# Counting gathered rows by half supersteps in the second edge loop of a two-layer graph network

## The chip, the cores and the metric

The kernel runs on one core of a Trainium2 chip. The metric is the time of one execution on the device in microseconds (us), lower is better. PE is the matrix engine (PEld its weight loads), DVE the vector engine, ACT the scalar engine, POOL the GpSimd engine, which here issues the indirect DMAs, and SP the engine that issues plain DMAs.

## What is computed

200,000 edges, sorted by destination, run between 12,500 nodes of 64 features. Cut to what matters, the reference is:

```
# layer 0
msg = relu(concat([x[dst], x[src], edge_attr, u[0]]) @ W1 + b1)
agg = segment_sum(msg, dst)
x   = layernorm(x + relu(concat([x, agg, u[0]]) @ W2 + b2))
# layer 1, 8 kinds of edges
Z   = einsum('ni,rio->nro', x, fc_weight)
e   = relu(sum(concat([Z[src, etype], Z[dst, etype]]) * attn_weight[etype]))
ex  = exp(e - segment_max(e, dst)[dst])
h   = segment_sum(ex / segment_sum(ex, dst)[dst] * Z[src, etype], dst)
x   = layernorm(x + h)
```

## The kernel before

**Tiles, slots, supersteps.** The edges are cut into NT = 1563 tiles of P = 128. The nodes are cut into NB = 98 blocks of 128. A tile whose edges end in more than one block is worked on once for each block; each such pair of a tile and a block is a slot. O = 8 slots are a superstep, and each loop runs over SO = 208 of them. The destinations that the reference draws make 1658 slots; the last six are filled up with the last tile. So the tile in the last slot of a superstep moves on by 8 from one superstep to the next, less one for every block that ends in between: counted from the drawn destinations it is tile 1510, 1517, 1525, 1532, 1539, 1546, 1553, 1560 and 1562 for supersteps 199 to 207.

**The two loops.** `phase_layer0` is the first loop, `phase_layer1` the second; `phase_mid` between them makes the tables of the second, and `phase_out` writes the result. In both, POOL runs `gathers`: for each tile in order one indirect DMA fetches the 128 source rows (table `Btab` or `Ztab`) into a ring of RING = 184 tiles, 23 supersteps' worth. POOL waits for the consumers only where a place of the ring is used again: for `used` and `summed`, which are PE's and DVE's progress some ten supersteps back.

**The count of landed rows.** In `gathers`, tiles are counted by eights (tiles 8g to 8g+7 are group g). Each gather adds 16 to one of four semaphores `s_g`, by its group. After the issue of the fourth tile of group g+1, `counted(g)` waits until all of group g has landed and adds 1 to the semaphore `landed`:

```
if s and j == min(3, NT - s * O - 1):
    counted(s - 1)
```

**Who waits for it.** A table `xrow` has four words for each superstep; word 0 is the group of the last slot's tile, plus 1. In the first loop DVE waits for it in `filled`. In the second PE waits for it in `scores(s)`, behind the first of 16 small matmuls into p_e:

```
if j == 0:
    e.wait_ge(S["landed"], e.snap(xreg, min_val=1, max_val=TO))
```

PE's order in one pass s of the second loop is `turned(s-1)` (p_x, from ACT's ohe), `scores(s+1)` (p_e), half of `summed(s-3)` (p_s from ohx), `spread(s-1)` (p_s from m), the other half of `summed(s-3)`. DVE does `scores`, `onehots(s+2)`, `maxima(s-1)`, `sums(s-4)`, `shifted(s-2)`. The tables `brow`, `wrow`, `xrow` are made once at the head of the first loop: DVE computes rows of `rowsf`, PE transposes them, DVE casts them to whole numbers.

Of the kernel before, what the change touches and what calls it, by code (L numbers as in the profile page):

```python
# [5 lines left out]
F32 = mybir.dt.float32  # L6
BF16 = mybir.dt.bfloat16
I32 = mybir.dt.int32
ALU = mybir.AluOpType
# [4 lines left out]
P = 128  # L14
# [7 lines left out]
NT = -(-E // P)  # L22
O = 8
TO = -(-NT // O)
# [4 lines left out]
SC = NS // P  # L29
# [46 lines left out]
CHUNKS = [(q, q + QC) for q in range(0, NQ, QC)]  # L76
# [356 lines left out]


ECHO = 8


def echoes(e, ping, echo, first):
# [4 lines left out]
            e.sem_inc(echo, 1)  # L443


def gathers(e, A, ring, table, idx, s_g, landed, used, summed, ping=None, echo=None, first=NT, free={}):

    tiles = lambda s: min(NT - s * O, O)


    def counted(s):
        e.wait_ge(s_g[s % len(s_g)], 16 * sum(tiles(i) for i in range(s % len(s_g), s + 1, len(s_g))))
        e.sem_inc(landed, 1)  # L453

    for t in range(NT):
        s, j = divmod(t, O)
        if s in free and j == 0:
            e.wait_ge(*free[s])
        if s >= RT and j == 0:
            e.wait_ge(used, s - RT + BEHIND + 1)  # L460

        if s >= RT and j in (2, 4, 6):
            e.wait_ge(summed, O * (s - RT + BEHIND - 1) + j)
        if j % 4 == 1 and t > first:
            e.wait_ge(echo, ECHO * ((t - first) // 4 + 1))
        e.indirect_dma_start(out=ring[:, place(t), :], out_offset=None, in_=table[:, :],  # L466
                             in_offset=bass.IndirectOffsetOnAxis(ap=idx[:, t:t + 1], axis=0)).then_inc(s_g[s % len(s_g)], 16)
        if j % 4 == 0 and t >= first:
            e.sem_inc(ping, 1)
        if s and j == min(3, NT - s * O - 1):  # L470
            counted(s - 1)
    counted(TO - 1)


def rows_loaded(e, A, drow, s_dr, made, g):
# [8 lines left out]
def phase_layer0(nc, A):  # L484

    QE, QO = 2, 3
    EARLY = 10 * O
    H = O // 2
    with ExitStack() as ctx:
# [3 lines left out]
        ring = sb("ring0", [P, RING, D], F32)  # L493
# [12 lines left out]
        xTA = ring[:, XT0:RING, :].rearrange("p (q h) d -> p q (h d)", h=2)  # L506

        rA = OH[:, :, :, :].rearrange("p a j k -> p (a j k)")[:, 0:2 * QC * 2 * D].rearrange("p (a q h d) -> p a q h d", a=2, q=QC, h=2)
        rowsf = sb("rows_f", [P, 6, SC], F32)

        rowi = msg[0:SC, :, :, :].rearrange("p a j d -> p (a j d)")[:, 0:3 * P + PER * WX].bitcast(I32)
        rowx = rowi[:, 3 * P:3 * P + PER * WX].rearrange("p (s w) -> p s w", w=WX)
# [16 lines left out]
        pre, tot = pM[:, 3, 256:256 + SC], pM[:, 3, 288:288 + SC]  # L529
        tab = pM[:, 3, P:P + 4 * SC].rearrange("p (m v) -> p m v", v=4)  # L530
        pR = pM[0:SC, 0, :].rearrange("p (r k) -> p r k", r=4)
        pR2 = pM[0:SC, 1, 0:2 * P].rearrange("p (r k) -> p r k", r=2)
        pL = [pM[:, 1 + i, :].bitcast(BF16).rearrange("p (m k) -> p m k", k=P) for i in range(2)]
        pY = lambda g: pM[:, 3 if g % 2 == 0 else 0, :].rearrange("p (m k) -> p m k", k=P)
        A3v = A.A3[:, 0:NB, :].rearrange("p (q h) c -> p q h c", h=2)
# [32 lines left out]

        @block.gpsimd
        def _(e):  # L570
            gathers(e, A, ring, A.Btab, idx, s_g, S["landed"], S["full"], S["acc"], S["ping"], S["echo"], EARLY, {XT0 // O: (T["a"], len(CHUNKS))})

        @block.scalar
        def _(e):
# [82 lines left out]
        def _(e):  # L657
# [49 lines left out]
            for r in range(4):  # L707
                e.transpose(pR[:, r, :], rowsf[:, r, :], A.ident[:, :])
            e.wait_ge(T["dh"], 8)
            for r in range(2):  # L710
                last = e.transpose(pR2[:, r, :], rowsf[:, 4 + r, :], A.ident[:, :])
            last.then_inc(T["rowt"], 1)
            multiplied(2)
# [44 lines left out]
        def _(e):  # L758
            breg = [e.alloc_register(f"l0vb{j}") for j in range(O)]
            treg = [e.alloc_register(f"l0vt{j}") for j in range(O)]  # L760
            xreg = [e.alloc_register(f"l0vx{j}") for j in range(WX)]
            done = Chain(e, T["dve"])
            c13 = lambda v: v.unsqueeze(2)

# [44 lines left out]
            done(e.tensor_scalar(out=rowsf[:, 5, :], in0=rowsf[:, 1, :], scalar1=float(O), scalar2=float(O), op0=ALU.is_ge, op1=ALU.mult))  # L809
            done(e.tensor_tensor(out=rowsf[:, 4, :], in0=rowsf[:, 5, :], in1=rowsf[:, 1, :], op=ALU.subtract))  # L810
            done(e.tensor_tensor(out=rowsf[:, 4, :], in0=rowsf[:, 4, :], in1=rowsf[:, 2, :], op=ALU.add))
            done(e.tensor_scalar(out=rowsf[:, 0, :], in0=tab[:, :, 1], scalar1=A.kcol[:, 0:1], scalar2=float(NB), op0=ALU.add, op1=ALU.min))
            done(e.tensor_scalar(out=nb128[:, :], in0=rowsf[:, 0, :], scalar1=-float(P), scalar2=None, op0=ALU.mult))
            e.sem_inc(T["rows"], 1)
# [8 lines left out]
            e.tensor_copy(rowx[:, :, 0:1], by(pR[:, 3, :])[:, :, O - 1:O])  # L823
            e.tensor_copy(rowx[:, :, 1:2], by(pR2[:, 0, :])[:, :, O - 1:O])
            e.tensor_copy(rowx[:, :, 2:3], by(pR2[:, 1, :])[:, :, O - 1:O])
            e.memset(rowx[:, :, 3:4], 0).then_inc(T["rowi"], 1)
            remainder(0)
            remainder(1)
            e.wait_ge(A.s_typ, 32)
# [38 lines left out]
                e.tensor_tensor(out=acc, in0=acc, in1=pS[s % 2][:, j:j + 1, :], op=ALU.add).then_inc(S["acc"], 1)  # L868

            def filled(s):  # L870
                e.wait_ge(S["landed"], e.snap(xreg[0], min_val=1, max_val=TO))
                if s:
                    e.wait_ge(S["pre"], s)
                of, to = e.snap(xreg[1], min_val=0, max_val=RING - O), e.snap(xreg[2], min_val=0, max_val=O)
                e.tensor_tensor(out=full[:, bass.ds(to, O), :], in0=owns, in1=ring[:, bass.ds(of, O), :], op=ALU.add).then_inc(S["full"], 1)  # L875
# [11 lines left out]
            for s in range(SO + 2):  # L887
                if s + 1 < SO:
                    onehots(s + 1)
                if s < SO:  # L890
                    if s:
                        e.wait_ge(S["msg"], s)
                    for h in range(2):
                        e.wait_ge(S[f"m{h}"], s + 1)
                        e.tensor_reduce(out=pT[:, h * H:(h + 1) * H, :], in_=half(h), axis=AXX, op=ALU.add).then_inc(T["dve"], 1)  # L895
                if s >= 2:
                    e.reg_load(breg, A.brow[0:1, (s - 2) * O:(s - 1) * O])
                if s < SO:
                    e.reg_load(xreg, xrow[0:1, s, :])
                    e.reg_load(treg, wrow[0:1, s, :])  # L900
                    filled(s)
                    take(e, T["dve"], 2)
                for j in range(O):
                    if s >= 2:
                        summed(s - 2, j)
                    if s < SO:
                        added(s, j)
# [341 lines left out]
def phase_layer1(nc, A):  # L1249

    QO, QT, QV = 7, 5, 4
    with ExitStack() as ctx:
# [42 lines left out]

        @block.gpsimd
        def _(e):
            gathers(e, A, ring, A.Ztab, idx, s_g, S["landed"], S["s"], S["acc"])

        @block.scalar  # L1300
        def _(e):
# [22 lines left out]
        @block.tensor  # L1324
        def _(e):
            breg = [e.alloc_register(f"l1pb{j}") for j in range(O)]
            treg = [e.alloc_register(f"l1pt{j}") for j in range(O)]
            ureg = [e.alloc_register(f"l1pu{j}") for j in range(O)]
            xreg = e.alloc_register("l1px")

            def scores(s):
                e.reg_load(breg, A.brow[0:1, s * O:(s + 1) * O])
                e.reg_load(treg, trow[0:1, s, :])
                e.reg_load(xreg, xrow[0:1, s, 0:1])
                e.wait_ge(S["oht"], s + 1)
                if s:
                    e.wait_ge(S["ev"], s)
                for j in range(O):
                    b = e.snap(breg[j], min_val=0, max_val=NB)
                    e.matmul(pE[:, j, :], OHT[:, s % QT, j, :], A.S23[:, bass.ds(b, 1), :], start=True, stop=False)  # L1340
                    if j == 0:
                        e.wait_ge(S["landed"], e.snap(xreg, min_val=1, max_val=TO))
                    t = e.snap(treg[j], min_val=0, max_val=RING - 1)
                    part = ring_s[:, bass.ds(t, 1), 2 * D + 2:2 * D + 5].rearrange("p a i -> p (a i)")
                    last = e.matmul(pE[:, j, :], A.ident_h[:, :], part.unsqueeze(2).to_broadcast([P, 3, R]), start=False, stop=True)  # L1345
                last.then_inc(S["e"], 1)

            def turned(s):
                e.wait_ge(S["ohe"], s + 1)
                for j in range(O):  # L1350
                    last = e.transpose(pX[:, j, :], OHe[:, s % 2, j, :], A.ident[:, :])  # L1351
                last.then_inc(S["x"], 1)

            def spread(s):
                e.wait_ge(S["m3"], s + 1)
                for j in range(O):
                    last = e.matmul(pB[s % 2][:, j, :], OHT[:, s % QT, j, :], m3[:, s % 2, j, :], start=True, stop=True)
                last.then_inc(S["b"], 1)

            def summed(s, h):  # L1360
                if h == 0:
                    e.reg_load(ureg, trow[0:1, s, :])
                    e.wait_ge(S["ohx"], s + 1)
                for j in range(4 * h, 4 * h + 4):
                    t = e.snap(ureg[j], min_val=0, max_val=RING - 1)
                    last = e.matmul(pS[s % 2][h][:, j % 4, :], OHx[:, s % 2, j, :], ring[:, bass.ds(t, 1), 0:D + 1], start=True, stop=True)  # L1366
                last.then_inc(S["s" if h else "s0"], 1)

            scores(0)
            for s in range(SO + 3):  # L1370
                if 1 <= s <= SO:
                    turned(s - 1)
                if s + 1 < SO:
                    scores(s + 1)
                if s >= 3:
                    summed(s - 3, 0)
                if 1 <= s <= SO:
                    spread(s - 1)
                if s >= 3:
                    summed(s - 3, 1)  # L1380
# [343 lines left out]
```

## Time and profile before

| | us |
|---|---|
| median of 3 runs | 5511.41 |
| lowest and highest of them | 5510.93, 5514.28 |
| span of the profiled execution, first to last instruction | 4190.6 |
| median less that span | 1320.8 |
| PE busy in the span | 3206.3 (77%) |
| DVE busy | 2985.6 (71%) |
| POOL busy | 3029.9 (72%) |
| ACT busy | 1278.0 (30%) |

The profile gives the span of its execution and no other time for it, so the median of the runs stands for what that execution took as a whole. The busy shares are averages over both loops and what lies around them; they don't say which engine sets the pace. The 1320.8 us are outside the first and the last instruction, and no view shows what fills them.

### The profile page before, as it was taken

The numbers are of one execution on the slowest core, as the hardware profiler recorded it, in microseconds if no ns is written. First come the engines' busy times: TensorE is split into PE (matmuls) and PEld (weight loads), VectorE is DVE, ScalarE is ACT, GpSimd is POOL, SyncE is SP. The second block draws the span as 40 slices with busy tenths as digits, with TensorE's granted clock in tenths as the row PEclk, the third lists the DMA queues.
The fourth block names the chain that finished last, engine by engine and source line by source line (L and its number), as shares of the span: only waits on it lengthen the run. The fifth ranks groups of instructions, "written<-read, shape, count | busy, mean of one in ns | idle before, by whom it ended". The sixth has DMA issues, their size and how long they took to land. (4 is left out here: it accounts for less than half of the span.)

```text
span 4190.6 us, 74370 instructions
## 1 busy us (share of the span) xinstructions
PE 3206.3 (77%) x17849; PEld 2851.7 (68%) x17849; DVE 2985.6 (71%) x9486; ACT 1278.0 (30%) x4181; POOL 3029.9 (72%) x3265
## 2 busy tenths in 40 slices
PE   6877677777677777777857877787878888888885
PEld 6766666667666766666626767676777777777774
DVE  6876676677677777777656666676767777777777
ACT  3000000000000000000334544555555555555555
POOL 5777777777777777777257777777777777777773
PEclk6555555555555555555775555555555555555555
DMA  5322222222222222222452222222222222222221
GB/s 187 104 71 71 60 71 71 69 63 72 70 71 72 65 69 71 72 71 62 151 209 59 49 59 49 59 59 59 49 59 59 59 59 49 59 59 59 59 49 37
DMA packets 172566, 300.35 MB, mean 72 GB/s; under 512 B 71720, under 2 KB 78236, under 8 KB 158845
## 3 DMA queue, kind: packets, MB, share of 16 engines
q0 software_dynamic: 100032, 105.03, 12.7%
q1 hardware_dynamic: 43526, 104.29, 6.9%
q10 hardware_dynamic: 28598, 86.26, 6.0%
q8 instruction: 173, 2.83, 0.3%
q14 instruction: 237, 1.93, 0.2%
HBM read 260.36 MB, written 34.99 MB: 70 GB/s over the span
## 5 line engine op out<-in xcount | busy, mean ns | idle before, releaser
L466 POOL DMA_INDIRECT ring<-Btab,idx x1563 | 1485.5, 950 | 504.6 <-issue 338.9
L466 POOL DMA_INDIRECT ring<-Ztab,idx x1563 | 1478.9, 946 | 485.6 <-issue 352.8
L1366 PE MATMUL p_s<-ring,ohx 128*128 x3328 | 806.3, 421 | 160.5 <-issue 157.0
L1366 PEld LDWEIGHTS p_s<-ring,ohx 128*128 128x128 f32 x3328 | 734.7, 325 | 180.8 <-issue 180.8
L754 PEld LDWEIGHTS p_s<-msg,oh 128*128 128x128 f32 x3328 | 726.2, 331 | 99.8 <-issue 99.7
L754 PE MATMUL p_s<-msg,oh 128*128 128x64 f32 x3328 | 756.9, 422 | 48.4 <-ACT msg L648 45.8
L741 PE MATMUL p_m<-A,oht 128*128 x1664 | 436.1, 364 | 411.0 <-DVE full L875 401.7
L648 ACT ACTIVATE msg<-p_t 128x512 f32<-128x512 f32 x208 | 124.2, 597 | 1803.8 <-DVE p_t L881 1790.9
L746 PE MATMUL p_m<-W1c,eaT 65*128 65x128 f32 x1664 | 573.9, 449 | 24.4 <-DMA eaT<-in_eaT_in 24.4
L741 PEld LDWEIGHTS p_m<-A,oht 128*128 128x128 bf16 x1664 | 233.4, 141 | 490.4 <-issue 444.4
L1454 DVE SCALAR_TENSOR_TENSOR XA<-XA,ff,p_s 128x65 f32 x1664 | 468.4, 281 | 129.9 <-DVE XA L1454 73.1
L1424 DVE TENSOR_REDUCE mslot<-p_x 128x8 f32<-128x1024 f32 x208 | 254.7, 1224 | 429.1 <-PE p_x L1351 427.7
L1315 ACT ACTIVATE ohe<-oh,ev 128x128 f32<-128x128 bf16 x1664 | 505.3, 386 | 44.6 <-DVE ev L1414 44.6
L1309 ACT ACTIVATE ohx<-oh,ex 128x128 f32<-128x128 bf16 x1664 | 508.7, 388 | 0.0
L1345 PE MATMUL p_e<-ring,ident_h 128*128 x1664 | 303.4, 196 | 234.2 <-POOLq L453 226.5
L746 PEld LDWEIGHTS p_m<-W1c,eaT 65*128 65x128 f32 x1664 | 455.9, 334 | 33.4 <-DMA eaT<-in_eaT_in 27.7
L875 DVE TENSOR_TENSOR full<-p_m,ring 128x512 f32 x208 | 143.6, 690 | 448.9 <-POOLq L453 430.3
L1351 PE MATMUL p_x<-ident,ohe 128*128 128x128 f32 x1664 | 397.6, 418 | 0.0
L1345 PEld LDWEIGHTS p_e<-ring,ident_h 128*128 128x128 bf16 x1664 | 166.6, 105 | 336.4 <-issue 274.0
L881 DVE TENSOR_TENSOR p_t<-p_t,full 128x64 f32<-128x64 f32 x1664 | 386.2, 233 | 11.7 <-issue 6.3
L868 DVE TENSOR_TENSOR XA<-XA,p_s 128x64 f32 x1664 | 366.9, 221 | 36.2 <-issue 8.5
L895 DVE TENSOR_REDUCE p_t<-p_m 128x256 f32<-128x768 f32 x416 | 379.5, 956 | 13.9 <-PE p_m L746 13.1
(212 smaller groups left out, 3084.4 us busy)
## 6 DMA issues: line engine op xcount, KB each, us to landing
drow<-drow_d SPq DMA_DIRECT2D x53, 1024.0 KB, 5.4
drow<-drow_d ACTq DMA_DIRECT2D x51, 1024.0 KB, 5.2
eaT<-in_eaT_in ACTq DMA_DIRECT2D x208, 128.0 KB
Ztab<-Z_stage SPq DMA_DIRECT2D x49, 536.0 KB, 5.5
ring<-Btab,idx POOLq DMA_INDIRECT x1563
ring<-Ztab,idx POOLq DMA_INDIRECT x1563
xTB<-in_xTB_in SPq DMA_DIRECT2D x7, 448.0 KB, 7.7
Btab<-B_stage SPq DMA_DIRECT2D x7, 448.0 KB, 5.1
```

The lines of the kernel that those rows point to most:

```text
L466: e.indirect_dma_start(out=ring[:, place(t), :], out_offset=None, in_=table[:, :], in_offset=bass.IndirectOffsetOnAxis(ap=idx[:, t:t + 1], ...
L741: e.matmul(parts(j), OHT[:, s % 2, j, :], A.A3[:, bass.ds(b, 1), :].rearrange("p a c -> p (a c)"), start=True, stop=True)
L746: last = e.matmul(own(j // 2), eaT[:, s % QE, j // 2, :], A.W1c2[:, :], start=True, stop=True)
L754: last = e.matmul(pS[r % 2][:, j, :], OH[:, r % QO, j, :], msg[:, r % 2, j, :], start=True, stop=True)
L881: ins = e.tensor_tensor(out=pT[:, j:j + 1, :], in0=pT[:, j:j + 1, :], in1=full[:, bass.ds(t, 1), :], op=ALU.add)
L895: e.tensor_reduce(out=pT[:, h * H:(h + 1) * H, :], in_=half(h), axis=AXX, op=ALU.add).then_inc(T["dve"], 1)
L1309: ins = e.activation(OHx[:, o, j, :], OH[:, s % QO, j, :], ACT.Copy, scale=ex[:, o, j:j + 1])
L1315: ins = e.activation(OHe[:, s % 2, j, :], OH[:, s % QO, j, :], ACT.Relu, scale=ev[:, s % QV, j:j + 1])
L1345: last = e.matmul(pE[:, j, :], A.ident_h[:, :], part.unsqueeze(2).to_broadcast([P, 3, R]), start=False, stop=True)
L1351: last = e.transpose(pX[:, j, :], OHe[:, s % 2, j, :], A.ident[:, :])
L1366: last = e.matmul(pS[s % 2][h][:, j % 4, :], OHx[:, s % 2, j, :], ring[:, bass.ds(t, 1), 0:D + 1], start=True, stop=True)
L1454: e.scalar_tensor_tensor(out=acc, in0=acc, scalar=ff[:, s % QV, j:j + 1], in1=pS[s % 2][j // 4][:, j % 4:j % 4 + 1, :], op0=ALU.mult, op1= ...
```

## The change

`gathers` gets the number of tiles that are counted together as an argument, `part`. The first loop passes O = 8 and keeps its count. The second passes HALF = 4: the semaphore of a gather goes by its group of four, and `counted(q)` for group of four q (tiles 4q to 4q+3) follows the issue of tile 4q+7. A new row `rowsf[:, 6, :]` is, for every slot, the group of four of its tile plus 1; it goes into word 3 of `xrow`, which was zero. The second loop's `scores` waits for word 3 in place of word 0. In both loops the word is first copied into a register `landed` by a register instruction.

```
-def gathers(e, A, ring, table, idx, s_g, landed, used, summed, ping=None, echo=None, first=NT, free={}):
+def gathers(e, A, ring, table, idx, s_g, landed, used, summed, part, ping=None, echo=None, first=NT, free={}):
-    def counted(s):
-        e.wait_ge(s_g[s % len(s_g)], 16 * sum(tiles(i) for i in range(s % len(s_g), s + 1, len(s_g))))
+    def counted(q):
+        e.wait_ge(s_g[q % len(s_g)], 16 * sum(tiles(i) for i in range(q % len(s_g), q + 1, len(s_g))))
         e.sem_inc(landed, 1)
...
-                             in_offset=bass.IndirectOffsetOnAxis(ap=idx[:, t:t + 1], axis=0)).then_inc(s_g[s % len(s_g)], 16)
+                             in_offset=bass.IndirectOffsetOnAxis(ap=idx[:, t:t + 1], axis=0)).then_inc(s_g[t // part % len(s_g)], 16)
...
-        if s and j == min(3, NT - s * O - 1):
-            counted(s - 1)
-    counted(TO - 1)
+        if (t - HALF + 1) % part == 0 and t >= part + HALF - 1:
+            counted((t - HALF + 1) // part - 1)
+    for q in range((NT - HALF) // part, -(-NT // part)):
+        counted(q)
...
-            for r in range(2):
+            for r in range(3):
                 last = e.transpose(pR2[:, r, :], rowsf[:, 4 + r, :], A.ident[:, :])
...
+            done(e.tensor_tensor(out=w[:, :], in0=rowsf[:, 1, :], in1=rowsf[:, 5, :], op=ALU.subtract))
+            done(e.tensor_scalar(out=w[:, :], in0=w[:, :], scalar1=float(HALF), scalar2=1.0, op0=ALU.is_ge, op1=ALU.subtract))
+            done(e.scalar_tensor_tensor(out=rowsf[:, 6, :], in0=rowsf[:, 3, :], scalar=2.0, in1=w[:, :], op0=ALU.mult, op1=ALU.add))
...
-            e.memset(rowx[:, :, 3:4], 0).then_inc(T["rowi"], 1)
+            e.tensor_copy(rowx[:, :, 3:4], by(pR2[:, 2, :])[:, :, O - 1:O]).then_inc(T["rowi"], 1)
...
                     e.reg_load(xreg, xrow[0:1, s, :])
+                    e.reg_alu(landed, xreg[0], 0, ALU.max)
...
-            gathers(e, A, ring, A.Ztab, idx, s_g, S["landed"], S["s"], S["acc"])
+            gathers(e, A, ring, A.Ztab, idx, s_g, S["landed"], S["s"], S["acc"], HALF)
...
-                e.reg_load(xreg, xrow[0:1, s, 0:1])
+                e.reg_load(xreg, xrow[0:1, s, 3:4])
+                e.reg_alu(landed, xreg, 0, ALU.max)
...
-                        e.wait_ge(S["landed"], e.snap(xreg, min_val=1, max_val=TO))
+                        e.wait_ge(S["landed"], e.snap(landed, min_val=1, max_val=2 * TO))
```

POOL at the end of the second loop, before; each row is one gather (`l1_g0` to `l1_g3` are `s_g`, `l1_s` is `used`, `l1_acc` is `summed`), and the last gather is tile 1562:

```order
L466 DMA ring<-Ztab,idx 128x67 [waits l1_g1,l1_acc]
L466 DMA ring<-Ztab,idx 128x67
L466 DMA ring<-Ztab,idx 128x67 [waits l1_acc]
L466 DMA ring<-Ztab,idx 128x67
L466 DMA ring<-Ztab,idx 128x67 [waits l1_s]
L466 DMA ring<-Ztab,idx 128x67
L466 DMA ring<-Ztab,idx 128x67 [waits l1_acc]
L1252 UNCONDITIONAL_BRANCH [waits l1_g2,l1_g3]
```

The same gathers of the changed kernel:

```order
L467 DMA ring<-Ztab,idx 128x67 [waits l1_g3,l1_acc]
L467 DMA ring<-Ztab,idx 128x67
L467 DMA ring<-Ztab,idx 128x67 [waits l1_acc]
L467 DMA ring<-Ztab,idx 128x67
L467 DMA ring<-Ztab,idx 128x67 [waits l1_g0,l1_s]
L467 DMA ring<-Ztab,idx 128x67
L467 DMA ring<-Ztab,idx 128x67 [waits l1_acc]
L1259 UNCONDITIONAL_BRANCH [waits l1_g1,l1_g2]
```

The wait for a count of gathers, which stood ahead of one gather in eight, now stands ahead of one in four; it is always for a tile five places back (tile 1555 ahead of tile 1560, in the added one).

PE in the middle of the second loop, from `turned` to the first matmuls of `scores`, before:

```order
L1351 MATMUL p_x<-ident,ohe 128x128 x7
L1332 TENSOR_LOAD tabs
L1333 TENSOR_LOAD tabs
L1334 TENSOR_LOAD tabs
L1339 ISA [waits l1_ev,l1_oht]
L1340 MATMUL p_e<-S,oht 128x24
L1343 ISA [waits l1_landed]
L1345 MATMUL p_e<-ring,ident_h 128x24
```

And the same place of the changed kernel:

```order
L1360 MATMUL p_x<-ident,ohe 128x128 x7
L1340 TENSOR_LOAD tabs
L1341 TENSOR_LOAD tabs
L1342 TENSOR_LOAD tabs
L1343 REGISTER_ALU
L1348 ISA [waits l1_ev,l1_oht]
L1349 MATMUL p_e<-S,oht 128x24
L1352 ISA [waits l1_landed]
L1354 MATMUL p_e<-ring,ident_h 128x24
```

One register instruction is added for each superstep, and the wait for `landed` keeps its place.

DVE at the head of the first loop, where the rows of the tables are made, in the changed kernel; the rows L815 to L817 are new:

```order
L812 TENSOR_SCALAR rows_f<-rows_f 128x13 [waits t_dve]
L813 TENSOR_TENSOR rows_f<-rows_f 128x13 [waits t_dve]
L814 TENSOR_TENSOR rows_f<-rows_f 128x13 [waits t_dve]
L815 TENSOR_TENSOR t_scan<-rows_f 128x13 [waits t_dve]
L816 TENSOR_SCALAR t_scan<-t_scan 128x13 [waits t_dve]
L817 SCALAR_TENSOR_TENSOR rows_f<-rows_f,t_scan 128x13 [waits t_dve]
L818 TENSOR_SCALAR rows_f<-p_m,kcol 128x13 [waits t_dve]
```

They stand between the row that was last of `rowsf` and the two behind it, each waiting for the one before.

## Rows read from the trace of the kernel before

**Rows 1.** Source line L466: duration min/median/max, first and last start, idle before.

```profile
L466 POOL DMA_INDIRECT ring<-Btab,idx x1563: 940/944/2818, 30.7 to 1992.4; - x196
L466 POOL DMA_INDIRECT ring<-Ztab,idx x1563: 940/944/1205, 2151.0 to 4105.2; - x196
```

**Rows 2.** Waits, 2250 to 4190 us: total, times, longest.

```profile
POOL ring L466 <- issue: 331.2, 1086, 0.5
PE p_e L1345 <- POOLq L453: 196.6, 121, 3.2
POOL ring L466 <- DVE XA L1454: 73.1, 240, 0.3
POOL ring L466 <- DMA ring<-Ztab,idx: 42.4, 139, 0.3
POOL ring L466 <- PE p_s L1366: 5.8, 19, 0.3
```

**Rows 3.** Timeline of POOL, end of the second loop: start, duration, idle before.

```profile
4091.45 0.94 POOL L466 DMA_INDIRECT ring<-Ztab,idx  x1 [0.30 <-issue]
...
4101.44 0.94 POOL L466 DMA_INDIRECT ring<-Ztab,idx  x1 [0.30 <-issue]
4102.69 0.94 POOL L466 DMA_INDIRECT ring<-Ztab,idx  x1 [0.30 <-issue]
4103.94 0.94 POOL L466 DMA_INDIRECT ring<-Ztab,idx  x1 [0.30 <-DMA ring<-Ztab,idx]
4105.18 0.94 POOL L466 DMA_INDIRECT ring<-Ztab,idx  x1 [0.30 <-DVE XA L1454]
```

**Rows 4.** Timeline of PE, the same stretch.

```profile
4072.09 1.91 PE L1351 MATMUL p_x<-ident,ohe 128*128 128x128 f32 x8
...
4084.02 0.20 PE L1345 MATMUL p_e<-ring,ident_h 128*128 x1 [1.27 <-POOLq L453]
...
4094.09 0.20 PE L1345 MATMUL p_e<-ring,ident_h 128*128 x1 [1.37 <-POOLq L453]
...
4104.02 0.20 PE L1345 MATMUL p_e<-ring,ident_h 128*128 x1 [1.30 <-POOLq L453]
...
4112.56 0.18 PE L1345 MATMUL p_e<-ring,ident_h 128*128 x1
...
4119.90 0.18 PE L1345 MATMUL p_e<-ring,ident_h 128*128 x1
...
4120.35 0.20 PE L1345 MATMUL p_e<-ring,ident_h 128*128 x1
4120.63 0.20 PE L1345 MATMUL p_e<-ring,ident_h 128*128 x1
```

**Rows 5.** Timeline of DVE, last sum of the loop, first of `phase_out`.

```profile
4152.90 0.28 DVE L1454 SCALAR_TENSOR_TENSOR XA<-XA,ff,p_s 128x65 f32 x1 [0.16 <-DVE XA L1454]
4153.51 0.25 DVE L1513 TENSOR_SCALAR den<-XA 128x98 f32<-128x98 f32 x1 [0.32 <-PEq L1252]
```

**Rows 6.** Timeline of POOL in the first loop, its longest wait.

```profile
123.45 0.94 POOL L466 DMA_INDIRECT ring<-Btab,idx  x1 [1.25 <-DMA ring<-Btab,idx]
```

**Rows 7.** Timeline of DVE and PE, head of the first loop.

```profile
45.39 0.17 DVE L810 TENSOR_TENSOR rows_f<-rows_f 128x13 f32<-128x13 f32 x1
45.71 0.17 DVE L811 TENSOR_TENSOR rows_f<-rows_f 128x13 f32<-128x13 f32 x1
...
69.99 3.25 PE L668 MATMUL p_s<-W1a,ring 64*128 64x64 f32 x28
```

**Rows 8.** Waits over the span: DVE in the first loop.

```profile
DVE full L875 <- POOLq L453: 430.3, 156, 4.3
```

**Rows 9.** Timeline of POOL between the loops: a small wait laid bare.

```profile
2017.33 0.60 POOL L1195 MEMSET S_parts<- 128x224 bf16 x1 [0.15 <-POOLq L50]
```

**Rows 10.** Page: span and count of instructions.

```profile
span 4190.6 us, 74370 instructions
```

More of the change, by code:

```diff
@@ L435 @@
 ECHO = 8
+HALF = O // 2
 def echoes(e, ping, echo, first):
@@ L443, in echoes @@
             e.sem_inc(echo, 1)
-def gathers(e, A, ring, table, idx, s_g, landed, used, summed, ping=None, echo=None, first=NT, free={}):
-    tiles = lambda s: min(NT - s * O, O)
-    def counted(s):
-        e.wait_ge(s_g[s % len(s_g)], 16 * sum(tiles(i) for i in range(s % len(s_g), s + 1, len(s_g))))
+def gathers(e, A, ring, table, idx, s_g, landed, used, summed, part, ping=None, echo=None, first=NT, free={}):
+    tiles = lambda q: min(NT - q * part, part)
+    def counted(q):
+        e.wait_ge(s_g[q % len(s_g)], 16 * sum(tiles(i) for i in range(q % len(s_g), q + 1, len(s_g))))
         e.sem_inc(landed, 1)
@@ L508, in phase_layer0 @@
         rA = OH[:, :, :, :].rearrange("p a j k -> p (a j k)")[:, 0:2 * QC * 2 * D].rearrange("p (a q h d) -> p a q h d", a=2, q=QC, h=2)
-        rowsf = sb("rows_f", [P, 6, SC], F32)
+        rowsf = sb("rows_f", [P, 7, SC], F32)
         rowi = msg[0:SC, :, :, :].rearrange("p a j d -> p (a j d)")[:, 0:3 * P + PER * WX].bitcast(I32)
@@ L531, in phase_layer0 @@
         pR = pM[0:SC, 0, :].rearrange("p (r k) -> p r k", r=4)
-        pR2 = pM[0:SC, 1, 0:2 * P].rearrange("p (r k) -> p r k", r=2)
+        pR2 = pM[0:SC, 1, 0:3 * P].rearrange("p (r k) -> p r k", r=3)
         pL = [pM[:, 1 + i, :].bitcast(BF16).rearrange("p (m k) -> p m k", k=P) for i in range(2)]
@@ L570, in _ @@
         def _(e):
-            gathers(e, A, ring, A.Btab, idx, s_g, S["landed"], S["full"], S["acc"], S["ping"], S["echo"], EARLY, {XT0 // O: (T["a"], len(CHUNKS))})
+            gathers(e, A, ring, A.Btab, idx, s_g, S["landed"], S["full"], S["acc"], O, S["ping"], S["echo"], EARLY, {XT0 // O: (T["a"], len(CHUNKS))})
         @block.scalar
@@ L761, in _ @@
             xreg = [e.alloc_register(f"l0vx{j}") for j in range(WX)]
+            landed = e.alloc_register("l0vn")
             done = Chain(e, T["dve"])
@@ L870, in filled @@
             def filled(s):
-                e.wait_ge(S["landed"], e.snap(xreg[0], min_val=1, max_val=TO))
+                e.wait_ge(S["landed"], e.snap(landed, min_val=1, max_val=TO))
                 if s:
@@ L1329, in _ @@
             xreg = e.alloc_register("l1px")
+            landed = e.alloc_register("l1pn")
             def scores(s):
```

## Prediction

> **What bounds the kernel now.** I first read the row of the one line that issues all gathers. In the second loop its first and last of 1563 gathers start at 2151.0 and 4105.2 us [rows 1]: 1954.2 us over 1562 steps, 1.251 us each. Its median duration is 0.944, so about 0.31 us lies between two. Then I asked the view of waits what that gap is. POOL's idle time in this loop is put down to issue, to DVE, to DMA and to PE, but the longest of any of the last three is 0.3 us [rows 2], the same as the gap ahead of a gather that waits for nothing [rows 3]. So POOL never stands still for a consumer: it runs at its own pace from first to last gather, and the reader should see that the waits named there cost nothing. PE, the other way, waits 121 times for POOL's count, 196.6 us in all [rows 2]. The loop is paced by POOL's 1563 gathers; earlier news of a landed tile cannot make it issue the next one earlier. What can change is the work left when POOL is done.
>
> **The end of the loop.** The tiles of the last slots (in the section on the kernel) say which group each superstep waits for. Tile 1562 is issued at 4105.18; going back by 1.25, tile 1559 is the row at 4101.44 and tile 1551 the one at 4091.45 [rows 3]. PE's scores of superstep 205 (last tile 1553, group 194, complete with tile 1559) are released at 4104.02, those of 204 (tile 1546, complete with 1551) at 4094.09 [rows 4]: 2.58 and 2.64 us after the start of the tile that completes the group. I take 2.6 us from start to count. Superstep 206 then starts at 4112.56 and 207 at 4119.90, neither released by POOL [rows 4]. Behind them the pipeline drains until the last sum at 4152.90, and the output phase follows at 4153.51 [rows 5]. So today the tail hangs on the release of 205 by tile 1559.
>
> **The change, part by part.**
>
> *The earlier release (the gain).* Of the 208 last tiles, 89 lie in the first four of their eight; those supersteps are released four tiles, 4 x 1.25 = 5.0 us, sooner, the rest at the same time as before. At the end these are 203 (tile 1539), 204 (1546), 205 (1553). 206 (1560) must in both kernels wait for tile 1562, which is counted at 4105.18 + 2.6 = 4107.8. From one release to the next unreleased start PE needs 4112.56 - 4104.02 = 8.5 us, and without a wait in front 4119.90 - 4112.56 = 7.3 [rows 4]. Superstep 202 (tile 1532) lies in the second four of its eight and keeps its time of some 4074.0: it follows the p_x matmuls, which start at 4072.09 and last 1.91 [rows 4]. After the change:
>
> 203: the later of 4079.0 (4084.0 less 5.0) and 4074.0 + 8.5 gives 4082.5; it was 4084.0. 204: the later of 4089.1 and 4091.0 gives 4091.0. 205: the later of 4099.0 and 4099.5 gives 4099.5. 206: the later of 4107.8 and 4108.0 gives 4108.0; it was 4112.5. 207: 4115.3 to 4116.5, by the step of 7.3 or 8.5; it was 4119.9. The gain at the last superstep is thus between 3.4 and 4.6 us; I take 4.2, nearer the unwaited step, since DVE has no one-hots left to build there, as it had none before. More than 4.8 it cannot be, because tile 1562 lands when it lands.
>
> *More counting on POOL.* There are 391 groups of four in place of 196 of eight: 195 more waits and 195 more increments. Today each such pair stands in front of one gather in eight, and the gap there is 0.30 us, as everywhere [rows 3]: the cost is hidden by the running gather, and I take 0. The cover is that POOL's instruction stream runs ahead of the gather in work: the wait for group 194 stands behind the issue of tile 1562 in the program, yet it released PE at 4104.02 [rows 4], before that tile started at 4105.18 [rows 3]. Every new wait asks for a tile five places back, like the old ones: 2.6 us to land, 6.2 us of gathers as cover. If it is gone, the gap grows as it did once in the first loop, to 1.25 us [rows 6]: 0.95 us for that once. The other end, with no cover for any, is 0.15 us, the gap that a bare small wait leaves on POOL [rows 9], times 195 = 29 us; it is a rival below.
>
> The Trainium skill, page "Advanced Engine Details and Errata", section "Network/Comms", gives 50 to 100 ns for a sequencer's reading of a semaphore; by it 195 more would be 10 to 20 us, if nothing hid them. The same page, section "Engine Queue Depths", gives GpSimd a queue of 8, which would be the cover; the trace agrees in that no old wait widens the gap of 0.30 us.
>
> *Register instructions.* One on PE per superstep of the second loop, one on DVE per superstep of the first. The trace names none. The late matmuls of scores follow each other by 4120.63 - 4120.35 = 0.28 us [rows 4] for two matmuls and two register instructions, so one is at most 0.07 us (below: nothing). In the loops PE and DVE wait for POOL anyway, DVE 430.3 us in 156 supersteps [rows 8], so they are hidden; if nothing hid them they would be 208 x 0.07 = 15 us a loop. At the tails they count: five supersteps of the second loop, 0.3 us, and two of the first, 0.1 us.
>
> *The new row of the table.* Three DVE instructions in a chain, at the pitch of their neighbours 45.71 - 45.39 = 0.32 us [rows 7]: 1.0 us, one transpose and a cast for a memset, 0.3 us at most by the same pitch. They delay the last multiplications that free the ring, which end at 69.99 + 3.25 = 73.2 [rows 7]. POOL wants those places at tile 80, which at (1992.4 - 30.7) / 1562 = 1.256 us a tile [rows 1] is 30.7 + 80 x 1.256 = 131 us. So 58 us of cover; cost 0.
>
> *Queues.* No DMA is added or moved; SP's and ACT's queues are as before.
>
> **The sum.** 4.2 gained, less 0.3 and 0.1: 3.8 us off the span of 4190.6, so 4186.8. With the 1320.8 us around it (median less span) this is 5507.6, against the median of 5511.4: -0.07%. A measurement of this kernel can tell about 0.2%, 11 us, from no change, so the forecast is: the same.
>
> **Rivals.**
>
> *A, the counting is laid bare (slower).* POOL's stream does not run ahead as far as I read, and each of 195 added pairs lengthens POOL's chain, which sets the pace, by 0.15 us. For it: POOL is the one engine whose delay goes straight to the end. Against it: 196 such pairs leave no trace today. It gives 29 - 4 = +25 us, 5537; it decides as soon as a pair costs over 0.08 us (15 us).
>
> *B, the time around the span grows.* 1320.8 us lie outside; if they go by the number of instructions, 208 + 208 + 390 + 5 = 811 more on 74370 [rows 10] are 1.1%, 14 us, net +10: 5522. Nothing shows what fills that time, so this can't be excluded; it ends at the edge of 0.2%.
>
> The Trainium skill, page "Runtime: NRT & Kernel Launch", puts the fixed cost of a launch near 15 us, by which the time around would not grow; no view here shows that time, and 1320.8 is far from it.
>
> *C, the release is on the pacing loop after all (faster).* If timed executions are not paced by POOL as the profiled one is, PE's shortened waits count: 89 of 208 supersteps, of which 121 in 208 wait, 1.62 us each (196.6 / 121 [rows 2]), is 84 us: 5427. Against it: POOL never waits over 0.3 us in this loop. It would need POOL to stand still for `used` or `summed`.
>
> *D, it does nothing.* Superstep 206 starts no earlier, because something but the releases sets the beat at the end. 5511.
>
> **Chances.** Forecast 0.72; A 0.07; B 0.07, a little over half of it beyond 0.2%; C 0.07; D 0.07. Faster: 0.07 (C). Slower: 0.07 + 0.04 = 0.11. The same: 0.82. The range leaves out A and C: from 5499, a bound of 4.8 us gained and the scatter of the runs shown (3.3 us) taken twice and rounded down, to 5521, B's net with nothing added.
>
> **What would show it.** POOL's last gather again 1954 us after its first, gaps of 0.30 (if 1983, A). PE's first p_e row with a release by POOL for 203 and 205 gone or shorter, 206 near 2.6 to 3 us behind the start of tile 1562 (before, 7.4), last sum about 44 us behind it instead of 47.7. PE's wait for POOL's count in total hardly smaller, because PE, released earlier, waits for the next count instead. The prediction is wrong if POOL's gaps widen, if POOL waits for PE or DVE, or if span and time move apart.

## The result and the profile after

In the runs of the first measurement the changed kernel took 5522.01 us (median of 20 runs, 5516.26 to 5535.84), the kernel before 5509.23 us (20 runs, 5502.72 to 5518.77). The ratio is 1.0024 [1.0018, 1.0031]: slower by 0.24%, 13 us. The forecast was 5507.6 and "the same", with a range up to 5521.

The page and five views of the profiled execution of the changed kernel (its own time is 5532.91 us). Of the page, the span and the busy times:

```profile
span 5531.2 us, 74989 instructions
PE 3114.4 (56%) x17850; PEld 2800.3 (51%) x17850; DVE 2989.8 (54%) x9489; ACT 1278.0 (23%) x4181; POOL 3024.8 (55%) x3265
```

Its line of gathers, with the first and last start of each loop:

```profile
L467 POOL DMA_INDIRECT ring<-Btab,idx x1563: 938/944/2037, 31.6 to 2645.5; - x196
L467 POOL DMA_INDIRECT ring<-Ztab,idx x1563: 938/944/1162, 2941.1 to 5333.5; - x196
```

Its waits from 2950 to 5500 us:

```profile
...
DVE mslot L1433 <- remote: 860.5, 174, 42.4
...
POOL ring L467 <- remote: 362.0, 172, 2.2
POOL ring L467 <- issue: 359.4, 1169, 0.5
...
PE p_e L1354 <- issue: 291.7, 278, 5.6
PE p_e L1349 <- issue: 283.2, 242, 21.1
...
```

Its timeline of POOL over one group of eight gathers, and of PE in the same scores:

```profile
4503.77 0.94 POOL L467 DMA_INDIRECT ring<-Ztab,idx  x1 [2.16 <-remote]
4505.02 0.94 POOL L467 DMA_INDIRECT ring<-Ztab,idx  x1 [0.30 <-issue]
...
4512.51 0.94 POOL L467 DMA_INDIRECT ring<-Ztab,idx  x1 [0.30 <-issue]
4515.59 0.94 POOL L467 DMA_INDIRECT ring<-Ztab,idx  x1 [2.13 <-remote]
```

```profile
4498.87 0.22 PE L1349 MATMUL p_e<-S,oht 128*128 x1
...
4510.72 0.22 PE L1349 MATMUL p_e<-S,oht 128*128 x1
...
4513.01 0.18 PE L1349 MATMUL p_e<-S,oht 128*128 x1 [1.25 <-issue]
4514.44 0.18 PE L1354 MATMUL p_e<-ring,ident_h 128*128 x1 [1.25 <-issue]
4515.16 0.18 PE L1349 MATMUL p_e<-S,oht 128*128 x1 [0.55 <-issue]
```

And its line of the sums over the second loop, the last of which ends the loop:

```profile
L1463 DVE SCALAR_TENSOR_TENSOR XA<-XA,ff,p_s x1664: 271/282/286, 3202.4 to 5493.5; 128x65 f32 x185
```

No engine is busy over 56%, so a wait sets the time, and the reader should see three things. First, span and time are 1.7 us apart (5532.91 - 5531.2), where the prediction had put 1320.8 us "around the span". The span of before [rows 10] was not a part of 5511 us; that trace shows an execution that is 1320 us shorter than the timed ones. Second, in this execution a step from gather to gather is (5333.5 - 2941.1) / 1562 = 1.53 us, not 1.25 [rows 1]. Each gather still takes 0.944 us and most gaps are still 0.30, but once in eight POOL stands still for more than 2 us. Something else is slower, and POOL waits for it. The view says `remote`, that is, it found the event that ended the wait but no instruction behind it; the program has one wait in eight gathers for `used`, which is PE's progress. Third, what is slower is PE: single matmuls of 0.18 us in the middle of the scores wait up to 1.25 us on "issue", that is for nothing that the profile shows, and the program has no wait at that place. From one superstep's scores to the next PE takes 4510.72 - 4498.87 = 11.85 us, and POOL's eight gathers take 4515.59 - 4503.77 = 11.82. PE's idle time on "issue" in this window is 854.8 us over its four lines (two of them are shown); before it was 159.0 from 2250 to 4190 us, nearly all in one row:

```profile
PE p_s L1366 <- issue: 153.1, 199, 0.9
```

Behind the last gather the last sum comes 5493.5 - 5333.5 = 160 us later, where before it was 47.7 [rows 3, 5]: PE and DVE are many supersteps behind POOL, so a tile has long landed when its superstep comes.

### The profile page after: what moved, and what is told of

The parts are those of the page before. It is cut to its first block and busy times, and to the rows that moved or that the text cites. A ratio compares the mean times of both kernels' runs of the same rounds, so it can differ in the third digit from the quotient of the medians.

```text
span 5531.2 us, 74989 instructions
## 1 busy us (share of the span) xinstructions
PE 3114.4 (56%) x17850; PEld 2800.3 (51%) x17850; DVE 2989.8 (54%) x9489; ACT 1278.0 (23%) x4181; POOL 3024.8 (55%) x3265
## 5 line engine op out<-in xcount | busy, mean ns | idle before, releaser
L756 PE MATMUL p_s<-msg,oh 128*128 128x64 f32 x3328 | 786.4, 409 | 784.3 <-issue 723.6
L756 PEld LDWEIGHTS p_s<-msg,oh 128*128 128x128 f32 x3328 | 753.0, 326 | 838.9 <-issue 838.7
L858 DVE TENSOR_TENSOR oh<-p_i,dstl 128x1024 f32<-128x1024 f32 x208 | 253.6, 1219 | 917.5 <-remote 909.0
L1349 PE MATMUL p_e<-S,oht 128*128 x1664 | 215.6, 191 | 386.8 <-issue 283.2
L1354 PE MATMUL p_e<-ring,ident_h 128*128 x1664 | 221.2, 186 | 295.8 <-issue 291.7
```

The source lines that it names most:

```text
L756: last = e.matmul(pS[r % 2][:, j, :], OH[:, r % QO, j, :], msg[:, r % 2, j, :], start=True, stop=True)
```

## Experiments

Six sets of runs were made on five chips. Each set has its own runs of the kernel before beside it, and these alone showed that the same kernel has two lengths:

| chip | before, median us (runs) | kind |
|---|---|---|
| 15 | 4192.34 (27) | short |
| 12 | 4191.78 (33) | short |
| 1 | 4191.45 (33) | short |
| 6 | 5583.85 (9) | long |
| 3, first set | 5592.9 (23) | long |
| 3, second set | 5512.37 (13) | long |

The trace of before [rows 10] is of the short kind, both medians of the first measurement are of the long one (its chip is not on record). The mean granted TensorE clock is the same in both kinds (0.520 in the trace of before, 0.519 in that of the changed kernel), so the clock does not separate them.

### Parts of the change on chips of the short kind

`e4_after` is the changed kernel. `e1_regs_only` is the kernel before with the register copies alone (in the first loop the same, on DVE):

```
+                e.reg_alu(landed, xreg, 0, ALU.max)
...
-                        e.wait_ge(S["landed"], e.snap(xreg, min_val=1, max_val=TO))
+                        e.wait_ge(S["landed"], e.snap(landed, min_val=1, max_val=TO))
```

`e3_count_only` is the changed kernel with counts by fours, but every superstep waits for the whole eight as before, so nothing is released earlier:

```
-            done(e.scalar_tensor_tensor(out=rowsf[:, 6, :], in0=rowsf[:, 3, :], scalar=2.0, in1=w[:, :], op0=ALU.mult, op1=ALU.add))
+            done(e.tensor_scalar(out=rowsf[:, 6, :], in0=rowsf[:, 3, :], scalar1=2.0, scalar2=float(-(-NT // HALF)), op0=ALU.mult, op1=ALU.min))
```

> The kernel before with nothing but the register copy of the awaited count, in both loops (416 register instructions). Theory R (the copies lengthen the chains of DVE and PE, which in a timed execution are not covered by POOL): all of the loss is here, ratio 1.0024 or about +13 us. Theory P (the 195 added counts on POOL cost): no change, ratio within 1.0006 of 1. Theory T (the earlier release shifts the beat of the second loop): no change. Its trace also shows whether a loop of this kernel takes 1954 us, as in the trace before, or near 2390 us as in the changed kernel's.

> The changed kernel, counting by fours on POOL, but each superstep of the second loop waits for the end of the whole group of eight as before (word 3 is twice word 0, at most 391), so nothing is released earlier. Theory R: +13 us, as the changed kernel. Theory P: +13 us too. Theory T: the share of the register copies alone, as e1. With e1 it tells the three apart.

> The changed kernel once more, beside the others on one chip: +13 us (ratio 1.0024) by its first measurement. All theories say the same; it is the level that e1 and e3 are held against.

The same three on chip 12:

> As e1, the register copies alone, once more, in case the executions are of the long kind (5510 us) this time: theory R +13 us there, theories P and T nothing. If they are of the short kind (4190 us): within 0.1% of the kernel before, as in e1.

> As e3, the counting by fours without the earlier release, once more. Long kind: theories R and P +13 us, theory T the share of f1 alone. Short kind: the same as the kernel before.

> The changed kernel once more. Long kind: +13 us. Short kind: 2 to 4 us faster than the kernel before, as in e4, since the tail behind POOL's last gather is 3.7 us shorter.

Measured: 0.9998 [0.9989, 1.0007], 1.0003 [0.9994, 1.0012] and 0.9992 [0.9983, 1.0001]. On chip 12 they gave 1.0001 [0.9992, 1.0010], 1.0002 [0.9993, 1.0011] and 0.9991 [0.9982, 1.0000].

The trace of `e4_after`: its line of gathers in the second loop, PE's waits for the count from 2250 to 4190 us, PE's releases of 205 and 206 by POOL, the last gather and the last sum:

```profile
L467 POOL DMA_INDIRECT ring<-Ztab,idx x1563: 940/944/1175, 2150.0 to 4104.9; - x196
```

```profile
PE p_e L1354 <- POOLq L454: 199.8, 124, 4.2
```

```profile
4098.81 0.20 PE L1354 MATMUL p_e<-ring,ident_h 128*128 x1 [1.20 <-POOLq L454]
...
4107.87 0.20 PE L1354 MATMUL p_e<-ring,ident_h 128*128 x1 [0.22 <-POOLq L454]
```

```profile
4104.87 0.94 POOL L467 DMA_INDIRECT ring<-Ztab,idx  x1 [0.30 <-issue]
```

```profile
4148.80 0.28 DVE L1463 SCALAR_TENSOR_TENSOR XA<-XA,ff,p_s 128x65 f32 x1 [0.16 <-DVE XA L1463]
```

Superstep 205 is released 6.1 us before tile 1562 starts, where it was 1.2 [rows 3, 4]. Superstep 206 is released by POOL itself, 3.0 us behind that tile's start; before it began 7.4 behind it. The last sum is 43.9 us behind it (before 47.7 [rows 3, 5]). In the trace of `e3_count_only`, which counts by fours but releases nothing earlier, the last gather starts at 4106.59 and the last sum at 4154.35: 47.8 us. On chip 12 the same distance is 43.8 us in `f4_after` and 47.2 in `f3_count_only`. So the whole gain is the earlier release. The 195 more waits on POOL cost nothing that can be measured: from first to last gather the second loop takes 1956.7 and 1954.6 us in `e3_count_only` and `f3_count_only`, 1954.1 and 1954.5 in `e1_regs_only` and `f1_regs_only`.

### The price of a register copy

> The kernel before with 16 register copies in place of one in each superstep of both loops (6656 register instructions in all). It measures the price of one and whether the loops have cover for them. If both loops are paced by POOL and a copy costs at most 0.07 us, 1.1 us a superstep is covered by the waits for POOL (1.6 to 2.8 us where there is one) and the time rises by under 10 us; if an execution is of the long kind, about 5510 us, where POOL waits for PE, then 416 x 16 copies at 0.02 to 0.07 us are paid, +130 to +460 us, and one copy would be 8 to 29 us of the 13.

`f5_regs16` repeats each copy 16 times. It gave 0.9998 [0.9989, 1.0007], which looks like "copies are free" and is not. The heads of the pages of `e1_regs_only` (one copy) and `f5_regs16` (16):

```profile
span 4189.3 us, 74786 instructions
```

```profile
span 4186.9 us, 74786 instructions
```

Both have 416 instructions more than before [rows 10]. So of identical copies in a row only one was executed; they must have become one when the program was built. `g1_pe128_before`, `g3_pe144_before` (128 and 144 copies on PE) and `g4_dve128_before` (128 on DVE) went the same way:

> The kernel before with the register copy, and in the second loop 128 copies on PE in each superstep in place of one: PE's instruction stream, not POOL, should set the pace, as it seems to in the long execution of the changed kernel. If a copy costs 0.03 to 0.07 us, a superstep of PE goes from some 8.5 to 12 to 17 us and the time rises by 400 to 1500 us; if it rises by under 10 us, the copies are covered even then and this is no stand-in. It is the level for the next two.

> The changed kernel with the same 128 copies on PE. Theory R (the one added copy is the loss where PE's stream paces): equal to g1, since both have the same number. Theory P or T (the counting by fours, or the earlier release, is the loss where PE paces): 13 us above g1 or more.

> As g1 with 144 copies: 16 x 208 = 3328 more. Theory R needs a price of 13 / 208 = 0.06 us for one, or 13 / 416 = 0.03 if both loops pay: +100 to +210 us on g1. A price under 0.01 us, +33 us or less, would refute it for PE.

> The kernel before with the register copy, and in the first loop 128 copies on DVE in each superstep in place of one. DVE is busy some 8 of 10 us there, so that its stream sets the pace if the copies are not covered: at 0.03 to 0.07 us each +4 to +9 us a superstep, less 2 us of cover, +400 to +1400 us in all. It gives the price of a copy on DVE.

The three on the kernel before have 74786 instructions each too, so they are three more runs of `e1_regs_only`: 1.0002, 1.0002 and 0.9999. `g2_pe128_after` is likewise the changed kernel again, 0.9993 [0.9984, 1.0002]. The rise of 100 us and more that was expected of them could not come, since no copies were added. With them the copies alone have six ratios on three chips, mean 1.0000, and the changed kernel three, mean 0.9992, which is -3 us of 4192; each of the three alone is at the edge of its interval. The price of one copy with no cover was not measured.

### PE made to set the pace

On chip 6 the transposes of the second loop were done three times, so that POOL must wait for PE there (5 runs of each kernel); `h1_pe3_before` has the register copies too, `h3_pe3_count` is `e3_count_only` so slowed:

```
-                for j in range(O):
+                for j in [j for k in range(3) for j in range(O)]:
```

> The kernel before with the register copy, and each of the 8 transposes into p_x in the second loop done three times (16 more matmuls of some 0.24 us, 3.8 us a superstep). This is real work for PE, which nothing can drop. PE then needs 8.5 + 3.8 = 12.3 us for a superstep against POOL's 10.0, so PE sets the pace and POOL waits: 208 x 12.3 = 2560 us for the loop in place of 1998, about 4750 us in all. It stands for an execution in which PE, not POOL, paces the second loop.

> The changed kernel with the same tripled transposes. Theory T or P (where PE paces, the earlier release or the counting by fours costs): above h1 by 0.2% or more, near 10 us. Theory that both are neutral there: within 3 us of h1, since PE never waits for the count and a release that comes before it is asked for is worth nothing; the tail gains nothing either.

> The counting by fours without the earlier release, with the same tripled transposes. Theory P: as h2, above h1. Theory T: as h1, below h2. Neutral: all three the same.

Measured against the plain kernel before: 1.0269 [1.0254, 1.0284], 1.0276 [1.0262, 1.0290], 1.0270 [1.0255, 1.0286]. The second loops of `h1_pe3_before`, `h2_pe3_after` and `h3_pe3_count`, from their lines of gathers:

```profile
L466 POOL DMA_INDIRECT ring<-Ztab,idx x1563: 942/947/1217, 2987.4 to 5495.7; - x196
```

```profile
L467 POOL DMA_INDIRECT ring<-Ztab,idx x1563: 938/944/1217, 2993.8 to 5500.5; - x196
```

```profile
L467 POOL DMA_INDIRECT ring<-Ztab,idx x1563: 942/947/1213, 2998.5 to 5507.5; - x196
```

They last 2508.3, 2506.7 and 2509.0 us; from the first gather to the last sum it is 2723.3, 2719.3 and 2722.7. The forecast of some 4750 us was missed because it reckoned with a chip of the short kind: chip 6 is of the long one, and 3328 more transposes added 156 us to 5583.85. Here the profile names the engine that POOL stands still for (`h1_pe3_before`, 3000 to 5500 us):

```profile
POOL ring L466 <- PE p_s L1370: 498.2, 129, 170.6
```

Where PE sets the pace, neither the counting by fours nor the earlier release nor the new row of the table, which only the last two kernels have, makes a difference that these runs can tell; their intervals reach 0.15% either way, 8 us.

### Parts of the change on a chip of the long kind

On chip 3 the copies alone and the whole change were timed beside each other (`k1_regs_only` is `e1_regs_only`, `k2_after` the changed kernel):

> The register copies alone beside it. Long kind: theory R +0.24%, the same as the changed kernel; theories P and T no change. Short kind: no change.

> The changed kernel on another chip. If that chip is of the long kind (5500 to 5600 us): +0.24% against the kernel before, as at first, if the loss goes with the change; nothing, if it went with the one chip. If it is of the short kind (4190 us): -0.08%, as in e4 and f4.

Measured: 1.0010 [1.0001, 1.0019] and 1.0019 [1.0010, 1.0028]. The lines of gathers of `k1_regs_only`, then of `k2_after`:

```profile
L466 POOL DMA_INDIRECT ring<-Btab,idx x1563: 938/944/2042, 30.6 to 2691.8; - x196
L466 POOL DMA_INDIRECT ring<-Ztab,idx x1563: 938/944/1165, 2987.8 to 5404.9; - x196
```

```profile
L467 POOL DMA_INDIRECT ring<-Btab,idx x1563: 941/947/2037, 31.6 to 2699.2; - x196
L467 POOL DMA_INDIRECT ring<-Ztab,idx x1563: 941/947/1165, 2995.3 to 5413.2; - x196
```

Two of PE's waits in the second loop of `k2_after` (3000 to 5500 us):

```profile
PE p_e L1354 <- issue: 318.7, 251, 5.7
...
PE p_e L1354 <- POOLq L454: 2.3, 1, 2.3
```

PE waits for POOL's count once, 2.3 us, where before in the short kind it waits 121 times [rows 2]. There is next to nothing left for an earlier release to shorten. The second loops are 2417.1 and 2417.9 us; the last sum comes 5565.4 - 5404.9 = 160.5 us behind the last gather in `k1_regs_only` and 5571.6 - 5413.2 = 158.4 in `k2_after`. The 6.2 us between the two profiled times (5604.89, 5611.10) lie in the first loop (2661.2 and 2667.6 us). The counting and the earlier release don't touch that loop. The copies alone were expected at +0.24% if they were the whole loss; at 0.10%, with an interval that ends at 0.19%, they are not shown to be.

The last pair asked which part of the rest costs. `l1_table_regs` is the changed kernel with neither counting by fours nor earlier release: the new row of the table and the copies are left.

```
-            gathers(e, A, ring, A.Ztab, idx, s_g, S["landed"], S["s"], S["acc"], HALF)
+            gathers(e, A, ring, A.Ztab, idx, s_g, S["landed"], S["s"], S["acc"], O)
...
-                e.reg_load(xreg, xrow[0:1, s, 3:4])
+                e.reg_load(xreg, xrow[0:1, s, 0:1])
```

`l2_count_only` is `e3_count_only` again.

> The changed kernel without its counting by fours and without the earlier release: what is left is the register copies, the new row of the table with its transpose, and the changed line of the count. Long kind: k1 gave +0.10% for the copies and k2 +0.19% for all; if the rest is the new row, this is at +0.19% as the whole change, if it is the counting on POOL, at +0.10%. Short kind: no change.

> The counting by fours with the copies and the new row, without the earlier release, as e3. Long kind: +0.19% if the earlier release plays no part there, since PE waits for the count only once (2.3 us in k2's trace); near 0 or above 0.3% if it does. Short kind: +0.03% as in e3 and f3.

Measured: 1.0030 [1.0019, 1.0041] and 1.0042 [1.0026, 1.0059], the latter from five runs; a sixth took 8789.96 us, is not in the ratio and has no explanation here. `l1_table_regs` is as slow as the changed kernel was in the first measurement (1.0024 [1.0018, 1.0031]) without any of what the change is named for; the second loops last 2391.3 and 2391.8 us in the two, 2392.4 in the changed kernel of the first measurement, and the tails up to the last sum 159.1, 159.9 and 160.0.

## Why the prediction was wrong

**What bounds the kernel (the step that failed).** "The loop is paced by POOL's 1563 gathers" is true of the execution that the trace of before shows, and of the chips of the short kind. It isn't true of the executions of the first measurement. There PE's issue sets the pace (11.85 us a superstep) and POOL stands still for over 2 us in one gather of eight. The sign lay open: a span of 4190.6 beside a median of 5511.4. The prediction took the 1320.8 us for time outside the span and carried them over unchanged. The changed kernel has 1.7 us there, and much the same has `e4_after` (4188.26 less 4186.5 is 1.8). With the right reading the prediction would have had no trace of the timed kind of execution, and a much wider range.

**The earlier release.** Where its premise holds it came out: forecast 3.4 to 4.6 us with 4.2 taken, 3.8 net; measured 3.8 at the last sum and -3 us over three comparisons. 205, forecast to be released at 4099.5, was released at 4098.81, 206 at 4107.87 for 4108.0, and PE's wait for the count stayed as long in total (199.8 after 196.6), as foreseen. In the long kind it is worth nothing that shows, since PE waits for a count once: the kernel without it (`l1_table_regs`) takes 2550.4 us from the first gather of the second loop to the last sum, the changed kernel of the first measurement 2552.4. Gains at a tail belong to the engine that arrives there last, and that was another engine.

**More counting on POOL.** Forecast 0, and in both kinds nothing was found: the ratios of `e3_count_only` and `f3_count_only` (1.0003, 1.0002), which hold the copies and the table too, and the second loops above, equal within 3 us. The gap of 0.30 us stayed. Rival A, at 29 us, is refuted.

**Register copies and the new row of the table (the terms that were mis-sized).** Forecast 0.4 us and 0. In the short kind that holds: 1.0000 over six comparisons for the copies. In the long kind the copies cost 0.10% [0.01, 0.19], with the row of the table it is 0.30% [0.19, 0.41], with the counting as well 0.42% [0.26, 0.59], and the whole change 0.19% [0.10, 0.28] and 0.24% [0.18, 0.31]. Their cover was that PE and DVE wait for POOL. If PE is the bound, the cover is gone; that this is why the copies cost is argued, not shown. The prediction had worked out this uncovered end (15 us a loop) but gave it neither a chance nor a place in the range. Its bound of 0.07 us a copy is not one either: it shares 0.28 us equally among two matmuls and two register instructions, and the row alone allows 0.14. 416 copies over the measured 13 us would be 0.03 us each; that is argued too, and it would leave nothing for the table.

**The rivals.** B had nearly the right time (5522, measured 5522.01) for a wrong reason: nothing lies outside the span, and 619 instructions were added, not 811. Added instructions do cost, but inside it. C supposed that PE paces timed executions and that shorter waits for the count would then be worth 84 us; the premise is right and the conclusion wrong, because a PE that sets the pace does not wait for the count. D, that the release does nothing, is what the long kind shows of the main edit.

**What stays open.** How the loss splits between the copies and the table: the two were measured in different sets of runs, between which the kernel before itself went from 5592.9 to 5512.37 us on the same chip, and the intervals only just touch. On chip 6, beside each other and with PE slowed, the whole change gave 1.0276 and the copies alone 1.0269, which speaks against a high price of the row. No run added other instructions at these places, so it isn't excluded that any small shift of PE's or DVE's program costs as much. Also where it arises. The differences between profiled executions lie in the first loop, but they are single profiles, and the runs of one kernel scatter by 10 us either way. An early start of the loss at the new row does not show: the store of the tables is issued at 147.29 us in `k1_regs_only`, which lacks the row, and with it at 148.22 in `k2_after` but at 146.77 in `l1_table_regs`; in `h1_pe3_before` and `h2_pe3_after` it is 147.21 and 147.45.

## What to carry to other kernels

Compare the span of the profile with the timed median first. If they differ by more than a few us, the trace shows another kind of execution than the one that is timed, and a claim on what sets the pace holds for the trace alone. An added instruction that is "hidden because its engine waits" should be priced once for the case that this engine is the bound, and that price belongs in the range with a chance. An experiment that repeats an instruction needs its count of instructions looked at before its time is believed.

## What the runs showed of the hardware

One program takes 4190 us on three chips and 5510 to 5600 us on two others, and what the traces show to differ is the issue on PE. At the head of the first loop the multiplications by `XA`, first in the long kind (the changed kernel of the first measurement), then in the short kind (`e4_after`):

```profile
74.68 0.27 PE L678 MATMUL p_m<-XA 128*128 128x128 bf16 x1 [2.53 <-issue]
77.48 0.26 PE L678 MATMUL p_m<-XA 128*128 128x128 bf16 x1 [2.54 <-issue]
```

```profile
44.96 5.49 PE L678 MATMUL p_m<-XA 128*128 128x128 bf16 x50 [0.81 <-DVE XA L808]
```

In the first, where it is slowest, one matmul starts every 2.80 us; in the second fifty are done in 5.49 us. With that the store of the tables is issued at 147.17 us in the one and at 52.63 in the other, and in the long kind stalls of 0.5 to 2 us return in both loops: in the first loop (200 to 2640 us) the matmuls of L756 wait 721.0 us on "issue", in `e4_after` (200 to 1990 us) that line waits 40.9 us, for ACT. Durations of single operations are the same (the gather's median is 0.944 us in both). Why the issue is slow on these chips, no view shows. The DMA transfers that bring instructions in blocks of 16 KB take about as long in both kinds (median 0.97 us in the changed kernel of the first measurement, 1.04 in `e4_after`), so it isn't those transfers that are slow. A chip was of the same kind in all of its runs, but for the one of 8789.96 us, and within the long kind the length on chip 3 moved by 1.5% from one set of runs to the next.
